# Causal attention over 1,024 rows: scores made once by query rows, four heads at a time, probabilities turned on TensorE

## The chip, the cores and the metric

The kernel runs on one core of a Trainium2 chip. The metric is device time in microseconds (us), the median of several executions. The core has TensorE (PE in the profile: matrix products and transposes, with weight loads listed as PEld), VectorE (DVE), ScalarE (ACT), GpSimd (POOL) and SyncE (SP, which here only issues DMAs). Each engine runs its own list of instructions strictly in the order written. Semaphores connect the lists.

## The reference, cut to what matters

```
x = L0_attn_x                                  # (4, 1024, 512)
xn = layernorm(x)
out = x + attn(xn) + ffn(xn)

def attn(x):                                   # 16 heads of 32
    q, k, v = split(x @ w_qkv)                 # 512 columns each
    q, k = rope(rmsnorm(q) * q_gamma), rope(rmsnorm(k) * k_gamma)
    scores = where(causal, q @ k.T / sqrt(32), -1e30)
    return (softmax(scores) @ v) @ w_out

def ffn(h):                                    # on 128 chosen rows of each batch
    idx = sort(top_k(h @ w_router, 128))
    x = h[idx]                                 # 512 rows in all
    ...                                        # attention of 16 heads of 128, and a gated MLP
    return h.at[idx].set(gate * processed + (1 - gate) * x)
```

## The kernel before, in words

The program has four stages on one core. First, rows are normalised and chosen for the FFN. Second, the attention of the chosen rows runs. Third comes their MLP, a loop of 16 steps in which PE is fed with weights split in a high and a low fp32r half. These three stages leave `delta`, what the FFN adds to its 512 rows. The fourth stage, which the change rewrites, is the attention over all 4 batches of 1,024 rows, written out by the functions `batch`, one for each engine.

For each batch PE first turns the normalised rows (L1154), and projects them tile by tile of 128 rows on q, k (L1176) and v (L1164) in plain fp32. DVE and POOL normalise and rope q and k: squares on ACT (L814), sums on DVE (L1479), the inverse root by a power on POOL (L597), scaling on DVE (L1490), and the sine products (L610 on POOL, L1502 on DVE). Then the tiles of the batch before get their output projection (`output`, L1097) plus one product with `onehotT` that puts `delta` on its rows (L1102).

The rest of a batch is a loop over 8 pairs of heads, each of 12 steps (`STEPS`), a step being a block of 128 keys against up to 512 queries. q and k are kept as stacks of a high part, a low part and a repeated high part, 96 rows (`STK`), so that one fp32r product has nearly fp32 precision. Row 97 of the q stack carries the negated row maximum. It is found one pair ahead, from scores made once more the other way round (`user` "max", L1079, seen by DVE at L1436 and L1440), turned on PE (L1084) and put in place by a small DMA. Scores then come out with keys on the partitions (L1118), ACT takes the exponent (L838), POOL blanks the part above the diagonal (L621), and PE multiplies by v and by ones in four column strips (L1142). DVE turns and inverts the sums and divides (L1449 to L1466). POOL splits the stacks of the pair after next (L578, L581), and PE turns them (L1072).

What runs beside a step is dealt out by the tables `BESIDE_Y` and `BESIDE_STEP`; banks of PSUM by `BANK`.

## Time and profile before

| | us |
|---|---|
| median of 3 runs | 1954.69 |
| lowest and highest run | 1952.83 and 1954.87 |
| profiled execution, first to last instruction (its span) | 1952.2 |
| PE busy in the span | 1766.3 |
| DVE busy | 1228.8 |
| ACT busy | 755.6 |
| POOL busy | 595.1 |

The page gives the profiled execution by its span. The runs are timed from outside the span, and the median stands 2.5 us above it. Busy time counts an engine's own instructions, and a matmul's entry reaches to its modelled end, so a full PE row does not mean that each column took the least time. What a matmul costs in a stream is read from the distance of starts.

### The profile page before, as it was taken

Reading aid. Unit: us, or ns where it says so; the run is one execution under the profiler, and the core shown is the slowest. Engines: PE = TensorE matmul, PEld = TensorE weight load, DVE = VectorE, ACT = ScalarE, POOL = GpSimd, SP = SyncE. Lnnn points to the kernel's source line nnn. Section 1 sums busy time; section 2 is a strip of 40 time slices with the busy share of each in tenths; the row PEclk is TensorE's granted clock in tenths of the full one; section 3 lists DMA queues with packets and bytes.
Section 4 is the critical chain, followed back from the end, with each engine's and each line's share of the span. In section 5 each row is a group of like instructions: output and inputs, shape, how many; then the busy total and the mean of one; then the engine's idle time right before and its main releaser. Section 6 shows DMA issues by size and latency. Waiting matters only on the chain.

```text
span 1952.2 us, 31482 instructions
## 1 busy us (share of the span) xinstructions
PE 1766.3 (90%) x9017; PEld 970.5 (50%) x9017; DVE 1228.8 (63%) x2797; ACT 755.6 (39%) x1682; POOL 595.1 (30%) x751
## 2 busy tenths in 40 slices
PE   0647999998998979999989999998999999899998
PEld 0435767666884445554435444444544444454443
DVE  6985656567984557775456777345677735467771
ACT  0002334332221126664124666312466531256652
POOL 1112010103443643331652332274233236422320
PEclk9878999999998969999999999999999999999999
DMA  7100112105331000001010000101000010100002
GB/s 249 54 1 22 33 32 64 32 16 180 99 104 43 0 1 2 2 2 44 1 54 34 2 2 2 45 1 54 34 2 2 2 46 0 65 23 2 2 2 87
DMA packets 55692, 70.43 MB, mean 36 GB/s; under 512 B 2680, under 2 KB 32048, under 8 KB 55536
## 3 DMA queue, kind: packets, MB, share of 16 engines
q1 hardware_dynamic: 55120, 67.20, 10.3%
q0 software_dynamic: 416, 1.34, 0.3%
q8 instruction: 75, 1.23, 0.3%
q14 instruction: 81, 0.66, 0.1%
HBM read 59.88 MB, written 8.39 MB: 35 GB/s over the span
## 4 chain that ended last, share of the span: by engine, by line
PE 71%; DVE 11%; ACT 7%; issue 7%; POOL 2%; DMA 1%; DVEq 0%; ACTq 0%; SPq 0%; POOLq 0%
PE psum L1142 13%; PE psum L1176 12%; PE psum L1079 9%; PE psum L1118 6%; PE psum L1097 5%; PE psum L1014 4%; PE psum L925 3%; PE psum L991 3%; ACT arena L838 3%; PE psum L1022 2%; PE psum L1072 2%; PE psum L935 2%; PE psum L969 2%; DVE arena L1490 2%; ACT k_stack L769 2%
## 5 line engine op out<-in xcount | busy, mean ns | idle before, releaser
L838 ACT ACTIVATE arena<-psum 128x512 f32<-128x512 f32 (+3 forms) x768 | 333.4, 488 | 247.0 <-PE psum L1118 245.9
L1440 DVE CUSTOM_DVE_ANT_0 psum<-psum,arena 128x128 f32<-128x128 f32 (+3 forms) x512 | 262.6, 527 | 211.3 <-PE psum L1079 205.8
L1142 PE MATMUL psum<-arena 128*32 128x512 f32 (+3 forms) x3072 | 326.1, 498 | 0.0
L1079 PE MATMUL psum<-k_stack,q_stack 96*128 96x512 f32 (+3 forms) x768 | 311.7, 438 | 11.3 <-ACT k_stack L769 7.6
L621 POOL TENSOR_SCALAR_AFFINE_SELECT arena<-arena 128x256 f32<-128x256 f32 x256 | 104.4, 408 | 498.7 <-ACT arena L838 498.7
L1079 PEld LDWEIGHTS psum<-k_stack,q_stack 96*128 96x128 f32 x768 | 139.2, 190 | 219.0 <-DVE arena L1436 72.6
L1176 PE MATMUL psum<-arena 128*128 128x512 f32 x512 | 227.2, 598 | 4.3 <-ACT arena L805 3.0
L1118 PE MATMUL psum<-q_stack,k_stack 97*128 97x512 f32 (+3 forms) x768 | 217.2, 364 | 0.2 <-DMA q_stack<-arena 0.2
L1436 DVE TENSOR_REDUCE arena<-psum 128x1 f32<-128x512 f32 x256 | 169.6, 687 | 28.4 <-PE psum L1079 28.2
L597 POOL TENSOR_TENSOR arena<-arena 128x32 f32<-128x32 f32 x32 | 173.8, 5431 | 2.8
L1176 PEld LDWEIGHTS psum<-arena 128*128 128x128 f32 x512 | 95.0, 190 | 134.2 <-issue 112.1
L1118 PEld LDWEIGHTS psum<-q_stack,k_stack 97*128 97x128 f32 x768 | 127.5, 190 | 49.5 <-ACT arena L838 37.1
L1097 PE MATMUL psum<-arena 128*128 128x512 f32 x256 | 132.9, 630 | 19.0 <-DVE arena L1490 16.4
L1072 PEld LDWEIGHTS psum<-ident_r,stack 128*96 128x96 f32 x1024 | 92.3, 127 | 93.4 <-issue 56.7
L1072 PE MATMUL psum<-ident_r,stack 128*96 128x128 f32 x1024 | 123.9, 246 | 12.5 <-POOL stack L581 12.4
L1506 DVE TENSOR_TENSOR arena<-arena 128x1024 f32<-128x1024 f32 x32 | 39.2, 1225 | 121.3 <-POOL arena L610 120.9
L1164 PE MATMUL psum<-arena 128*128 128x512 f32 x256 | 114.4, 592 | 0.0
L814 ACT ACTIVATE psum<-psum 128x1024 f32<-128x1024 f32 x32 | 32.3, 1008 | 210.8 <-PE psum L1176 210.8
L1479 DVE TENSOR_REDUCE arena<-psum 128x32 f32<-128x1024 f32 x32 | 39.2, 1224 | 97.1 <-ACT psum L814 97.1
L769 ACT ACTIVATE k_stack<-psum 96x512 fp32r<-96x512 f32 x128 | 77.6, 606 | 48.0 <-PE psum L1072 48.0
L527 POOL TENSOR_TENSOR k_stack<-arena,k_stack 128x512 fp32r<-128x512 f32 (+1 forms) x24 | 39.7, 1680 | 182.1 <-ACT k_stack L684 182.1
L1142 PEld LDWEIGHTS psum<-arena 128*32 128x32 f32 x3072 | 60.9, 108 | 67.1 <-issue 43.9
(161 smaller groups left out, 2562.3 us busy)
## 6 DMA issues: line engine op xcount, KB each, us to landing
arena<-in_L_attn_x SPq DMA_DIRECT2D x8, 2048.0 KB, 8.1
arena<-in_L_attn_x SPq DMA_DIRECT2D x16, 512.0 KB, 5.0
out_y<-arena SPq DMA_DIRECT2D x16, 512.0 KB, 2.7
arena<-in_L_ffn_wq SPq DMA_DIRECT2D x8, 512.0 KB, 4.5
arena<-in_L_ffn_wo SPq DMA_DIRECT2D x8, 512.0 KB, 4.0
arena<-in_L_ffn_w_gate SPq DMA_DIRECT2D x16, 256.0 KB, 2.9
arena<-in_L_ffn_w_up SPq DMA_DIRECT2D x16, 256.0 KB, 3.5
arena<-in_L_ffn_w_down SPq DMA_DIRECT2D x16, 256.0 KB, 2.6
```

Of the source, the lines that this page charges most:

```text
L597: pool.tensor_tensor(rs3[:, t % 2, :], ms3, half_neg, ALU.pow).then_inc(rs3_ready, 1)
L769: act.activation(dst, psum[0:RH, bank, :], ACT.Copy).then_inc(stackT_ready, 1)
L838: act.activation(probT[:, k % SLOTS, h, lo:CH], psum[:, (2 * k + h) % 3, lo:CH], ACT.Exp).then_inc(sc_exp, 1)
L1072: last = pe.transpose(psum[0:RH, bank, i * P:(i + 1) * P].bitcast(f32r), stack[:, w, t, h * STK:h * STK + RH], ident_r[:, :])
L1079: pe.matmul(psum[:, bank, 0:w], qS[p % 2][0:RH, t // 4, h * CH + t % 4 * P:h * CH + (t % 4 + 1) * P], kS[p % 2][0:RH, h, c * CH:c * CH + w ...
L1097: pe.matmul(bank, oT[:, g, t * P:(t + 1) * P], w_out[:, g, :], start=(g == 0), stop=False)
L1118: pe.matmul(psum[:, m % 3, lo:CH], kS[p % 2][0:RH + 1, h, j * P:(j + 1) * P], qS[p % 2][0:RH + 1, c, h * CH + lo:(h + 1) * CH], start=True ...
L1142: last = pe.matmul(psum[AD * r:AD * (r + 1), bank, lo:CH], w, probT[:, k % SLOTS, h, lo:CH], start=(j == 0), stop=(j == 4 * c + 3))
L1164: last = pe.matmul(psum[:, 4 + t % 2, :], xnT[:, k, t * P:(t + 1) * P], w_qkv[:, k, 2 * D:3 * D], start=(k == 0), stop=(k == KD - 1))
L1176: last = pe.matmul(psum[:, 2 * (t % 2) + w, :], xnT[:, k, t * P:(t + 1) * P], w_qkv[:, k, w * D:(w + 1) * D], start=(k == 0), stop=(k == K ...
L1436: dve.tensor_reduce(past, psum[:, bank, :], AX.X, ALU.max).then_inc(m_seen, 1)
L1440: dve.tensor_tensor_reduce(psum[:, bank, 0:w], psum[:, bank, 0:w], mask[:, CH - w:CH], 1.0, past if c else -3e38, ALU.add, ALU.max, top[:, ...
```

## The change

The last stage becomes 16 units (`U`), each a batch and four heads (`GH`). A unit has 24 pieces (`NPC`): for query tiles 0 to 3 two pieces of two heads each, for tiles 4 to 7 four pieces of one head. All engines walk the same loop over `i`, from `FIRST` (24 before the first piece) to `END`; the text calls a turn of it a slot, numbered 0 to 23 within its unit. In a slot:

- PE makes the scores of piece `i` with queries on the partitions, up to 1,024 keys wide, plus one product of `ident_r` with `limit` that sets the part above the diagonal (`score`). DVE takes the minimum of the negated scores (`least`), ACT the exponent with its sum (`probs`) into one of three `prob` buffers.
- PE turns the probabilities of piece `i - 2` in 128 x 128 blocks ("tA", "tB"), DVE and ACT copy them to `pT`.
- By the tables `STACK_AT`, `VALUE_AT`, `OUT_AT`, `XN_AT`, `QKV_AT` slots also hold the turned stacks of a coming query tile ("q", "k"), the values of a finished one ("o"), with the inverted sums spread by four more products, its output projection ("y", added by DVE to `y` in SBUF), for the first unit of a batch the turned x tiles ("x"), and one tile of the next unit's q, k, v projection ("w"). That projection is now three fp32r products of split operands, 384 columns wide. `w_qkv` is split by ACT and POOL during the MLP loop (`split_high`, `split_low`) and parked in DRAM.
- The next unit's q and k are normalised and roped in four chunks of two tiles: `rope3` on POOL, with the sums (`sums3`) and the scaling (`scale3`) on DVE in the slots of `SUMS_AT` and `SCALE_AT`.

The items "q" to "w" share four PSUM banks, dealt by `deal_banks`; `freed` makes PE wait until the item that had the bank before was read out. The product with `onehotT` goes; instead POOL adds `delta` to the rows of the output in DRAM by one indirect DMA for each batch, after the batch was written (`add_delta`). Loading x for the stage now waits until `delta` is done, since the memory is laid out anew.

```diff
+            def rope3(c):
+                u, cc = divmod(c, 4)
+                pool.wait_ge(raw_out, 2 * c + 2)
+                wait(pool, ss_made, c)
+                raw_c = raw3[:, c % 2].rearrange("p t n -> p (t n)")
+                pool.tensor_tensor(rot3, raw_c, raw_c, ALU.mult).then_inc(sq_made, 1)
+                pool.wait_ge(ss_made, c + 1)
+                wait(pool, rs_made, c)
+                pool.tensor_scalar(ms3, ss3[:, c % 2, :], 1.0 / AD, RMS_EPS, ALU.mult, ALU.add).then_inc(ms_made, 1)
+                pool.wait_ge(ms_made, c + 1)
+                pool.tensor_tensor(rs3[:, c % 2, :], ms3, half_neg[:, 0:16], ALU.pow).then_inc(rs_made, 1)
+                pool.wait_ge(scaled, c + 1)
+                wait(pool, lo_made, c)
+                src = raw3[:, c % 2].rearrange("p t (w h d) -> p (t w) h d", w=2, d=AD)
+                cos = cosG[:, 2 * cc:2 * cc + 2].rearrange("p t w d -> p (t w) d")
+                sin = sinG[:, 2 * cc:2 * cc + 2].rearrange("p t w d -> p (t w) d")
+                made = roped3.rearrange("p (a h d) -> p a h d", a=4, d=AD)
+                rot = rot3.rearrange("p (a h d) -> p a h d", a=4, d=AD)
+                half = AD // 2
+                pool.tensor_tensor(made, src, cos.unsqueeze(2).to_broadcast([P, 4, GH, AD]), ALU.mult)
+                for h in range(2):
+                    o = h * half
+                    last = pool.tensor_tensor(rot[:, :, :, o:o + half], src[:, :, :, half - o:AD - o],
+                                              sin[:, :, o:o + half].unsqueeze(2).to_broadcast([P, 4, GH, half]), ALU.mult)
+                last.then_inc(turned, 1)
+                pool.wait_ge(turned, c + 1)
+                pool.tensor_tensor(roped3, roped3, rot3, ALU.add).then_inc(roped_made, 1)
+                pool.wait_ge(roped_made, c + 1)
+                wait(pool, stack_ps, 2 * ((u - 1) * NT + 2 * cc + 2))
+                own = hl[:, 2 * cc:2 * cc + 2]
+                dst = own.rearrange("p t w h e d -> p (t w h) e d")
+                flat = roped3.rearrange("p (a d) -> p a d", d=AD)
+                parts = roped3.rearrange("p (t w h d) -> p t w h d", t=2, w=2, d=AD)
+                pool.tensor_copy(dst[:, :, 0, :], flat).then_inc(hi_made, 1)
+                for w in range(2):
+                    pool.tensor_copy(own[:, :, w, :, 2 - w, :], parts[:, :, w])
+                pool.wait_ge(hi_made, c + 1)
+                for w in range(2):
+                    last = pool.tensor_tensor(own[:, :, w, :, 1 + w, :], parts[:, :, w], own[:, :, w, :, 0, :].bitcast(f32), ALU.subtract)
+                last.then_inc(lo_made, 1)
...
+            def probs(i):
+                s, t, heads = piece(i)
+                w = (t + 1) * P
+                act.wait_ge(min_made, i + 1)
+                if i >= 3:
+                    act.wait_ge(tA_ps, i - 2)
+                    wait(act, tB_ps, seconds(i - 3))
+                wait(act, recip_made, s - 1)
+                for a, h in enumerate(heads):
+                    bank = 2 * (i % 2) + a
+                    src = psum[:, bank:bank + 2, :].rearrange("p a n -> p (a n)")[:, 0:w] if t >= 4 else psum[:, bank, 0:w]
+                    act.activation(prob[:, i % 3, a * CH:a * CH + w], src, ACT.Exp, bias=nmax[:, i % 4, a:a + 1], scale=-1.0,
+                                   accum_out=den[:, s % 2, h:h + 1]).then_inc(prob_made, 1)
...
+            def score(i):
+                s, t, heads = piece(i)
+                w = (t + 1) * P
+                wait(pe, prob_made, exps(i - 2))
+                pe.wait_ge(q_out, s + 1)
+                pe.wait_ge(k_out, s + 1)
+                for a, h in enumerate(heads):
+                    bank = 2 * (i % 2) + a
+                    if t >= 4:
+                        pe.matmul(psum[:, bank, :], qT[0:STK, s % 2, h, :], kT[0:STK, h, 0:CH], start=True, stop=True)
+                        bank, w0 = bank + 1, CH
                     else:
+                        w0 = 0
+                    pe.matmul(psum[:, bank, 0:w - w0], qT[0:STK, s % 2, h, :], kT[0:STK, h, w0:w], start=True, stop=False)
+                    last = pe.matmul(psum[:, bank, w - w0 - P:w - w0], ident_r[:, :], limit[:, :], start=False, stop=True)
+                last.then_inc(s_ps, 1)
...
+            def value(s):
+                u, t = divmod(s, NT)
+                bank = BANK_OF["o", s]
+                freed("o", s)
+                pe.wait_ge(recip_made, s + 1)
+                for h in range(GH):
+                    pe.matmul(psum[AD * h:AD * (h + 1), bank, P:2 * P], rden[:, s % 2, h:h + 1].to_broadcast([P, AD]), ident, start=True, stop=True)
+                pe.wait_ge(tA_out, end_of(s) + 1)
+                wait(pe, tB_out, seconds(end_of(s)))
+                pe.wait_ge(v_out, s + 1)
+                for j in range(t + 1):
+                    for h in range(GH):
+                        last = pe.matmul(psum[AD * h:AD * (h + 1), bank, 0:P], v[:, u % 2, j, h * AD:(h + 1) * AD], pT[:, s % 2, j, h, :],
+                                         start=(j == 0), stop=(j == t))
                 last.then_inc(o_ps, 1)
...
+            def project3(n):
+                u, m = divmod(n, NT)
+                bank = BANK_OF["w", n]
+                freed("w", n)
+                pe.wait_ge(w_in[u % 2], 16 * (u // 2 + 1))
+                pe.wait_ge(x_hi, u // 4 * NT + m + 1)
+                pe.wait_ge(x_lo, u // 4 * NT + m + 1)
+                for k in range(KD):
+                    for a, c in PARTS:
+                        last = pe.matmul(psum[:, bank, 0:3 * P], xnT[:, a, k, m * P:(m + 1) * P], w_s[u % 2][:, c, k, :],
+                                         start=(k == 0 and a + c == 0), stop=(k == KD - 1 and a == 1))
+                last.then_inc(w_ps, 1)
+            for i in range(FIRST, END):
...
+            def least(i):
+                s, t, heads = piece(i)
+                w = (t + 1) * P
+                bank = 2 * (i % 2)
+                dve.wait_ge(s_ps, i + 1)
+                if i >= 4:
+                    dve.wait_ge(prob_made, exps(i - 4))
+                if t < 4:
+                    dve.tensor_reduce(nmax[:, i % 4, :], psum[:, bank:bank + 2, 0:w], AX.X, ALU.min).then_inc(min_made, 1)
+                else:
+                    dve.tensor_reduce(nmax[:, i % 4, 0:1], psum[:, bank:bank + 2, :].rearrange("p a n -> p (a n)")[:, 0:w], AX.X, ALU.min).then_inc(min_made, 1)
...
+            def sums3(c):
+                dve.wait_ge(sq_made, c + 1)
+                wait(dve, rs_made, c - 1)
+                dve.tensor_reduce(ss3[:, c % 2, :], rot3.rearrange("p (h d) -> p h d", d=AD), AX.X, ALU.add).then_inc(ss_made, 1)
+            def scale3(c):
+                dve.wait_ge(rs_made, c + 1)
+                src = raw3[:, c % 2].rearrange("p t (h d) -> p (t h) d", d=AD)
+                dve.tensor_tensor(src, src, rs3[:, c % 2, :].unsqueeze(2).to_broadcast([P, 16, AD]), ALU.mult).then_inc(scaled, 1)
+            for i in range(FIRST, END):
+                if 0 <= i < U * NPC:
+                    least(i)
+                for kind, n in ring_items(i):
+                    if kind == "tA":
+                        first_out(n)
+                if recip_of(i) is not None:
+                    invert(recip_of(i))
+                for kind, n in ring_items(i - 1):
+                    if kind == "o":
+                        divide(n)
+                    if kind == "y":
+                        add_out(n)
+                    if kind == "x":
+                        x_low(n)
+                if turned_of(i, NORM_AT) is not None:
+                    normalise3(turned_of(i, NORM_AT))
+                if chunk_of(i, SUMS_AT, ()) is not None:
+                    sums3(chunk_of(i, SUMS_AT, ()))
+                if chunk_of(i, SCALE_AT, (0,)) is not None:
+                    scale3(chunk_of(i, SCALE_AT, (0,)))
...
+PROJECT, PROJECT_OUT, ROPE = (1, 3, 5), (2, 4, 6), (3, 5, 7)
+U = B * AH // 4
+GH = 4
+PIECES = [(t, (2 * a, 2 * a + 1)) for t in range(4) for a in range(2)] + [(t, (h,)) for t in range(4, NT) for h in range(GH)]
+NPC = len(PIECES)
+LAG = 2
+ENDS = [max(p for p in range(NPC) if PIECES[p][0] == t) for t in range(NT)]
...
+STACK_AT = {0: 1, 2: 2, 4: 3, 6: 4, 10: 5, 14: 6, 18: 7, 23: 8}
+VALUE_AT = {4: 0, 6: 1, 8: 2, 10: 3, 14: 4, 18: 5, 22: 6, 2: 7}
+OUT_AT = {6: 0, 8: 1, 10: 2, 12: 3, 16: 4, 20: 5, 0: 6, 4: 7}
+XN_AT = {1: 0, 2: 1, 4: 2, 6: 3, 8: 4, 10: 5, 12: 6, 15: 7}
+NORM_AT = {0: 0, 1: 1, 3: 2, 5: 3, 7: 4, 9: 5, 11: 6, 14: 7}
+QKV_AT = {3: 0, 5: 1, 7: 2, 9: 3, 11: 4, 13: 5, 16: 6, 19: 7}
+SUMS_AT = {7: 0, 11: 1, 15: 2, 21: 3}
+SCALE_AT = {10: 0, 14: 1, 18: 2, 0: 3}
+RECIP_AT = {3: 0, 5: 1, 7: 2, 9: 3, 13: 4, 17: 5, 21: 6, 1: 7}
...
+def ring_items(i):
+    s, out = stack_of(i), []
+    if s is not None:
+        out += [("q", s), ("k", s)]
+    if 0 <= i - LAG < U * NPC:
+        out.append(("tA", i - LAG))
+        if PIECES[(i - LAG) % NPC][0] > 1:
+            out.append(("tB", i - LAG))
+    for kind, n in (("o", value_of(i)), ("y", out_of(i)), ("x", turned_of(i)), ("w", projected_of(i))):
+        if n is not None:
+            out.append((kind, n))
     return out
...
+FIRST, END = -NPC, U * NPC + 6
+HELD = {"q": 0.6, "k": 0.8, "tA": 0.7, "tB": 0.6, "o": 1.5, "y": 1.5, "x": 1.5, "w": 1.0}
+def deal_banks():
+    free, holder, bank_of, before = [0.0] * 4, [None] * 4, {}, {}
+    for i in range(FIRST, END):
+        items = ring_items(i)
+        for n, (kind, idx) in enumerate(items):
+            k = min(range(4), key=lambda m: free[m])
+            bank_of[kind, idx] = 4 + k
+            before[kind, idx] = holder[k]
+            holder[k] = (kind, idx)
+            free[k] = i + n / max(4, len(items)) + HELD[kind]
+    return bank_of, before
+BANK_OF, BEFORE = deal_banks()
```

**DVE, between the scaling of one piece of q and k and the sums of the next.** Before, tile by tile in the projection, where `sums(t + 1)` stands ahead of the scaling of tile t:

```order
L1479 TENSOR_REDUCE arena<-psum 128x32 [waits ms3_ready,qk_sq]
L1490 TENSOR_TENSOR arena<-psum,arena 128x1024 [waits rs3_ready]
L1497 TENSOR_TENSOR arena<-arena 128x512 [waits scaled]
L1497 TENSOR_TENSOR arena<-arena 128x512
L1502 TENSOR_TENSOR arena<-arena 128x16x16 x2
L1506 TENSOR_TENSOR arena<-arena 128x1024 [waits cosed,rotated]
```

Now, from `scale3` of chunk 0 in slot 10 to `sums3` of chunk 1 in slot 11 of a unit:

```order
L1460 TENSOR_TENSOR raw<-raw,rs 128x512 [waits rs_made]
L1399 TENSOR_REDUCE nmax<-psum 128x1 [waits prob_made,s_ps]
L1412 COPY pT<-psum 128x4x128 [waits o_ps,tA_ps]
L1424 TENSOR_TENSOR oT<-psum,rdT 128x128 [waits y_ps,rdT_made]
L1434 TENSOR_TENSOR y<-psum,y 128x512 [waits y_added,y_ps]
L1454 TENSOR_REDUCE ss<-rot 128x16 [waits rs_made,sq_made]
```

The sums stood ahead of the scaling and waited for ACT's squares. They now stand one slot behind the scaling of the chunk before and wait for `sq_made`, POOL's squares.

**POOL, one tile of rope before, one chunk now.** Before:

```order
L595 TENSOR_SCALAR arena<-arena 128x32 [waits scaled,rs3_ready,ss3_ready]
L597 TENSOR_TENSOR arena<-arena 128x32 [waits ms3_ready]
L610 TENSOR_TENSOR arena<-arena 128x16x16 [waits roped_ready,scaled]
L610 TENSOR_TENSOR arena<-arena 128x16x16
```

Now, from the moment that a chunk is scaled to the power of the next chunk:

```order
L615 TENSOR_TENSOR roped<-raw,cosG 128x512 [waits lo_made,scaled]
L618 TENSOR_TENSOR rot<-raw,sinG 128x16x16 x2
L622 TENSOR_TENSOR roped<-roped,rot 128x512 [waits turned]
L629 CAST hl<-roped 128x16x32 [waits roped_made]
L631 CAST hl<-roped 128x2x4x32 x2
L634 TENSOR_TENSOR hl<-roped,hl 128x2x4x32 [waits hi_made]
L634 TENSOR_TENSOR hl<-roped,hl 128x2x4x32
L601 TENSOR_TENSOR rot<-raw 128x512 [waits ss_made,raw_out]
L604 TENSOR_SCALAR ms<-ss 128x16 [waits rs_made,ss_made]
L606 TENSOR_TENSOR rs<-ms,half_neg 128x16 [waits ms_made]
```

POOL had two sine products between a scaling and its next power. It now has the whole rope and the split of the stacks, eight instructions, and then the squares of the next chunk for which DVE waits.

**PE, a place in the loop over steps before, and slot 14 now.** Before:

```order
L1118 MATMUL psum<-q_stack,k_stack 128x512
L1079 MATMUL psum<-k_stack,q_stack 128x512
L1079 MATMUL psum<-k_stack,q_stack 128x128
L1142 MATMUL psum<-arena 32x512 x4
L1084 MATMUL psum<-arena 8x128
```

Now:

```order
L1085 MATMUL psum<-kT,qT 128x512
L1089 MATMUL psum<-kT,qT 128x256
L1090 MATMUL psum<-limit,ident_r 128x128
L1118 MATMUL psum<-ident_r,hl 96x128 x8
L1108 MATMUL psum<-consts,prob 128x128 x6
L1128 MATMUL psum<-consts,rden 32x128 x4
L1134 MATMUL psum<-pT,v 32x128 x20
```

Products of 512 columns in the strips (32 weight columns) gave way to products of 128 columns, and turned probabilities (L1108) stand where the second scores (L1079) stood.

## Rows read from the trace of the kernel before

**Rows 1.** The page, part 1: busy us, share of the span, instructions.

```profile
PE 1766.3 (90%) x9017; PEld 970.5 (50%) x9017; DVE 1228.8 (63%) x2797; ACT 755.6 (39%) x1682; POOL 595.1 (30%) x751
```

**Rows 2.** The chain that ended last, in time: start us, us, what, instructions.

```profile
207.16 5.31 PE psum L935 x48
...
459.93 2.75 PE psum L1014 x12
...
600.82 2.41 DVE arena L1399 x4
...
917.37 14.01 PE psum L1176 x32
...
1586.19 14.01 PE psum L1176 x32
...
1918.16 3.43 PE psum L1097 x8
```

**Rows 3.** Windows: length, busy us and count by engine, then PE's granted clock.

```profile
700.00:731.00 31.00, 21.62 (x88) 14.11 (x88) 19.96 (x50) 11.86 (x28) 10.45 (x17) 0.50 0.00 1
...
1055.00:1239.90 184.90, 182.43 (x1342) 88.81 (x1344) 130.72 (x348) 116.57 (x281) 51.27 (x111) 1.00 0.01 3
1240.20:1250.00 9.80, 6.26 (x29) 4.96 (x28) 2.35 (x4) 3.52 (x6) 0.81 (x4) 0.65 0.03 8
```

**Rows 4.** Timeline of PE inside a pair: start us, us.

```profile
1101.67 0.48 PE L1072 MATMUL psum<-ident_r,stack 128*96 128x128 f32 x4
1101.99 0.58 PE L1118 MATMUL psum<-q_stack,k_stack 97*128 97x384 f32 x2
...
1102.75 0.43 PE L1142 MATMUL psum<-arena 128*32 128x128 f32 x8
1103.11 0.48 PE L1072 MATMUL psum<-ident_r,stack 128*96 128x128 f32 x4
```

**Rows 5.** Timeline of PE, the last three steps of strips (384, 256, 128 columns).

```profile
1907.98 1.50 PE L1142 MATMUL psum<-arena 128*32 128x384 f32 x24
```

**Rows 6.** Timeline of PE, eight fp32 transposes in a row.

```profile
161.56 1.03 PE L885 MATMUL psum<-arena 128*128 128x128 f32 x8
```

**Rows 7.** Groups of DVE by shape: busy us, mean ns, idle before.

```profile
L1436 DVE TENSOR_REDUCE arena<-psum 128x1 f32<-128x512 f32 x256 | 169.6, 687 | 28.4 <-PE psum L1079 28.2
...
L1479 DVE TENSOR_REDUCE arena<-psum 128x32 f32<-128x1024 f32 x32 | 39.2, 1224 | 97.1 <-ACT psum L814 97.1
```

**Rows 8.** Groups of ACT by shape.

```profile
L838 ACT ACTIVATE arena<-psum 128x512 f32<-128x512 f32 x384 | 206.8, 590 | 141.6 <-PE psum L1118 141.3
...
L814 ACT ACTIVATE psum<-psum 128x1024 f32<-128x1024 f32 x32 | 32.3, 1008 | 210.8 <-PE psum L1176 210.8
...
L702 ACT ACTIVATION_READ_ACCUMULATOR arena<-arena 128x1 f32 x64 | 12.1, 190 | 0.0
```

**Rows 9.** Groups of POOL by shape.

```profile
L597 POOL TENSOR_TENSOR arena<-arena 128x32 f32<-128x32 f32 x32 | 173.8, 5431 | 2.8
...
L581 POOL TENSOR_TENSOR stack<-arena,stack 128x256 fp32r<-128x256 f32 x120 | 86.6, 742 | 9.5 <-POOL stack L578 8.2
L610 POOL TENSOR_TENSOR arena<-arena 128x256 f32<-128x256 f32 x64 | 49.1, 787 | 9.9 <-DVE arena L1490 9.9
L578 POOL CAST stack<-arena 128x256 fp32r<-128x256 f32 x120 | 45.0, 404 | 155.5 <-PE psum L1072 147.1 <-DVE arena L1506 8.4
L533 POOL TENSOR_TENSOR k_stack<-arena,k_stack 128x512 fp32r<-128x512 f32 x32 | 41.0, 1305 | 61.6 <-ACT k_stack L730 61.6
...
L494 POOL TENSOR_TENSOR arena<-arena 128x8 f32<-128x8 f32 x4 | 6.8, 1702 | 0.3
```

**Rows 10.** The page, part 6: DMA issues, KB each, us to landing.

```profile
arena<-in_L_attn_x SPq DMA_DIRECT2D x8, 2048.0 KB, 8.1
...
out_y<-arena SPq DMA_DIRECT2D x16, 512.0 KB, 2.7
```

1043 lines of the change are left out of this document (429 added, 614 removed).

## The prediction

> **What bounds the kernel now.** I read the page first for who is busy, then the chain that ended last for where time goes, then windows and a close timeline for what a product costs. PE is busy for 1766 of 1952 us, DVE for 1229 [rows 1]. The chain says where the last stage begins: DVE ends its last sum at 600.8 + 2.4 = 603.2 us, so the rewritten stage has 1349 of the 1952 us, and a batch costs (1586.2 - 917.4) / 2 = 334.4 us [rows 2]. In the pairs of a batch PE is busy for 182.4 of 184.9 us [rows 3]. So PE bounds the stage, and the question is whether it gets less to do and still gets it in time. Busy time doesn't tell the first, since an entry lasts longer than its place in a stream. I price PE by distances of starts.
>
> **Prices on PE.** An fp32r product of 512 columns costs 2.75 / 12 = 0.229, one of 128 costs 5.31 / 48 = 0.111 [rows 2]; between them I interpolate at the same slope (256: 0.122, 384: 0.176). An fp32 product of 512 columns is two instructions of 3.43 / 8 = 0.429, together 0.858 [rows 2]. Eight fp32 transposes end within 1.03 [rows 6]; without the last one's drain that is near the 0.111 of a 128-column product with its own weight load, and I take 0.11. Four fp32r transposes of a stack start 0.32 before what follows [rows 4]. Four strips of 128 columns (eight instructions) hold PE for 1103.11 - 1102.75 = 0.36 when they stand alone [rows 4]. Three steps in a row with 768 columns end within 1.50, or 1.43 without the 0.07 by which the entry in rows 4 outlasts its place; so each further 128 columns cost (1.43 - 0.36) / 5 = 0.21 [rows 5]. I take 0.22 and keep 0.36 as the other bound.
>
> How much the prices leave out I read from the pairs: scores 8 x 4.4, second scores and turned stacks 7 x 6.7, strips 8 x 10.5 make about 169 us, and with 184.9 us for some 430 groups of instructions [rows 3] a change of group costs 0.036.
>
> **PE's work in one of the 16 units.** Scores: 4 heads x (8 x 0.111 for the diagonal, 4 x 0.229, twice 0.638 for the odd widths) = 12.3. Turned probabilities: 36 blocks x 4 heads x 0.11 = 15.8. Turned stacks: 16 x 0.32 = 5.1. Values: 8 groups, 8 x 0.36 + 36 x 0.22 = 10.8, with the spread sums as one block each. Output: 8 x 0.858 = 6.9. Projection: 8 tiles x 12 x 0.176 = 16.9. Turned x: 0.9 on average. That is 68.7 us, and 118 groups x 0.036 = 4.2 beside. Four units make 292 us against the 334.4 of a batch now. By PE's work alone the change wins 12% of the stage: it drops the second scores and ones, and three fp32r products replace four passes of fp32, which outweighs the turned probabilities.
>
> **What the other engines have to do in a unit.** DVE: a reduction costs 0.687 at 512 and 1.224 at 1,024 [rows 7], so 0.15 + 1.05 per 1,000 columns; 24 minima over 18,432 columns are 23 us, 24 copies out 15.7, the rest 16, together 55. ACT: 0.17 + 0.82 per 1,000 columns, and 0.19 for reading each sum [rows 8]: 32 exponents 27 to 30, copies 26, together 55. POOL: a chunk of `rope3`. A 512-wide product costs 1.31, a 256-wide one 0.74 to 0.79, a cast of 256 0.40 and so of 512 about 0.67, and the power 1.70 for 8 and 5.43 for 32, so 2.95 for 16 [rows 9]. None of them is above PE's 73 in sum. The order is what matters.
>
> **The wait that the order makes.** After `scale3` of a chunk POOL must do the cosine product 1.3, two sine products 1.6, the sum 1.3, the cast 0.67, two copies 0.8, two subtractions 1.5, and only then the squares of the next chunk, 1.3, in all 8.8 with 0.35 for its own waits. `sums3` of the next chunk needs those squares, and stands on DVE one slot behind the scaling, for chunks 1 (slot 11 after 10) and 2 (slot 15 after 14). A slot of PE is 2.9 us on average. DVE has four instructions there, 2.5 us. So DVE stands still for 5 to 6 us twice a unit. Queued behind the sums are `least` and `first_out` of the next slot: ACT's exponents wait for the first, PE's banks for the second.
>
> I walked PE, DVE and ACT from there with the prices above and `deal_banks`' order. Time 0 is the end of the sums in slot 11. While DVE stood, PE did slot 12 and the start of 13 and then stopped, because "tB" of slot 13 lies in the bank of "tA" of slot 12, not copied yet: 3.6 us lost. DVE then needs 7.1 us to reach the scaling in slot 14; the squares and sums take 9.5; PE meanwhile ends slot 16 and stops before "tA" of slot 17, whose bank again waits for `first_out`: 4.3 us lost. Then 5.6 us to the scaling in slot 18, and 10.4 to the sums in slot 21, which find their squares ready, since three slots lie between. From there PE leads: its slots 22 to 9 are 35.7 us of work, group changes 2.2, x 0.5, 2.1 for slots 7 and 9, in which "w" takes the bank of the same slot's "tA" and waits for `least` and the copy; slot 10 up to its scaling 3.0, less 2.6 that PE was ahead: 40.9. And 9.6 back to time 0. The circle is 7.1 + 9.5 + 5.6 + 10.4 + 40.9 + 9.6 = 83.1 us a unit. Checked from PE's side: 68.7 + 4.2 + 7.9 + 2.9 for banks (the two slots above, and slot 11) = 83.7.
>
> **The ends.** The stage may load x only once `delta` is made: 603.2 + 1.9 for four multiplications that before came after the first normalised tile. What goes from the row choice (the turned one-hot matrix, about 2 us of PE and ACT) and what the splitting of `w_qkv` adds to the MLP loop (ACT and POOL have gaps there, but the chain through DVE is tight: 0 to 6 us) I set against each other. x and the first 1.5 MB of weights land about 8.3 us later, from 8.1 for 2 MB [rows 10]: 613.5. Two tiles projected at the 1.2 GHz that a pause leaves (half clock, as in [rows 3]) and copied out: 8.1, so 621.6. Squares and sums 2.1, then three chunks of 13.7 (power 3.2, scaling 0.7, 8.8, sums 0.7, handovers 0.3), since DVE reaches slot 0 only after the sums of chunk 3: 664.8. From the like point of unit 14 there are 2.9 us to its end. Unit 15 projects nothing: 50.9 + 4 for groups + 4 for banks and slots too short for DVE and ACT = 59. Its tail (last copies, values, division, projection) is 8, the output lands in 2.7 [rows 10], and the indirect DMA, for which no row exists, I set at 5, between 2.7 and 9: together 16.
>
> **Sum.** 664.8 + 15 x 83.1 + 2.9 + 59 + 16 = 1989 us of span, against 1952.2; with the 2.5 us by which the median of the runs stands above the span, 1992. The change is even with the kernel before at (1952.2 - 664.8 - 77.9) / 15 = 80.6 us a unit. Each us in a unit is 15 in the whole.
>
> **Rivals.** (1) Faster, because DVE's stop is covered: if PE runs further ahead than I let it, or POOL's eight steps take less. Half of the 7.9 us saved gives 79.1 a unit and 1932; all of it leaves 68.7 + 4.2 + 3.4 = 76.3 and 1890. It decides from 1.25 us less in each of the two gaps. For it: POOL's rows hold waits for the port and for data, DVE's are means over longer chains. Against it: POOL's products lie close to 0.74 and 1.31 in 120 and 32 instances [rows 9], and five of the eight steps are chained. Chance 0.33, faster in each form.
>
> (2) Slower still, because the clock falls in the gaps. The clock was at half for 31 us when PE was busy for 21.6 of them, and 0.65 in the 9.8 us that begin with a pause of 3.5 us and go on with 28 transposes [rows 3]. The gaps here are 3.6 and 4.3 us. One such fall in a unit, 6.8 us at half speed, costs 3.4, so 51 us: 2043. Against it: the gaps hold parts of products of 384 columns at both sides. Chance 0.17. The Trainium skill (TensorE: Matmul & The Clock Gate, Part 4: PE-mode transpose) states that transposes don't count as a busy PE in the way products do. [...] By that rule 21 of the 68.7 us would not count here, and the fall would be likelier.
>
> (3) Slower, because small strips don't stream: weights of 32 columns are loaded for each 128 columns, not for 512. At 0.36 for every block a unit costs 5.0 more: 2072. For it: the only steps in a row in the trace are wide ones [rows 5]. Chance 0.10.
>
> **How the numbers follow.** My own case holds 0.40, with 1965 to 2020 from POOL's chain at 8.0 to 9.5. The range 1885 to 2075 takes in the covered case at its lower end and the third rival at its upper end and leaves about 0.2 out. About 0.2% is what a measurement of this kernel can tell from no change. Faster 0.34, within 0.2% 0.04, slower 0.62.
>
> **What would show it.** In the changed kernel's trace DVE's sums (L1454) wait for POOL's squares (L601) by 5 to 6 us, twice a unit, and PE has gaps of about 4 us before L1108 in slots 13 and 17. Units come every 83 us. Strips (L1134) start 0.22 apart per block. If the sums wait for less than 2 us, the second part of my argument is wrong, and the time is near 1900.

## The result, and the profile after

The changed kernel takes 2020.19 us, the median of 5 runs from 2008.11 to 2025.24, against 1954.81 for the kernel before. The ratio is 1.0334, 95% interval 1.0305 to 1.0363: slower by 3.3%. The forecast was 1992, range 1885 to 2075, with a chance of 0.62 for slower; the median lies at the upper end of what the forecast gave its own case (1965 to 2020). The profiled execution is the shortest of the five (2008.11 us, span 2006.2). That matters below.

The page of the changed kernel, parts 1 and 5, answers to [rows 1] and [rows 7, 9]:

```profile
PE 1675.8 (84%) x14233; PEld 1366.2 (68%) x14233; DVE 1241.0 (62%) x2293; ACT 927.1 (46%) x2363; POOL 865.4 (43%) x940
...
L615 POOL TENSOR_TENSOR roped<-raw,cosG 128x512 f32<-128x512 f32 x64 | 81.6, 1275 | 323.5 <-DVE raw L1460 323.5
...
L606 POOL TENSOR_TENSOR rs<-ms,half_neg 128x16 f32<-128x16 f32 x64 | 186.4, 2913 | 5.3
...
L1454 DVE TENSOR_REDUCE ss<-rot 128x16 f32<-128x512 f32 x64 | 43.6, 682 | 161.4 <-POOL rot L601 161.4
```

PE is busy for 90 us less than before, and the whole is longer. DVE's sums stood still for 161.4 us behind POOL's squares. No share in part 1 shows it: POOL is busy 43% of the time. It is late at two places in each unit. The table of waits gives the number of times and the longest, and what came of it on PE:

```profile
DVE ss L1454 <- POOL rot L601: 161.4, 34, 7.8
...
PE psum L1108 <- DVE pT L1412: 92.6, 54, 3.7
...
PE psum L1166 <- DVE pT L1412: 53.2, 42, 6.3
```

One unit's second wait, on the timeline of DVE (start us, us, and idle time before it in brackets):

```profile
1141.04 0.68 DVE L1460 TENSOR_TENSOR raw<-raw,rs 128x512 f32<-128x512 f32 x1
1142.71 0.96 DVE L1399 TENSOR_REDUCE nmax<-psum 128x1 f32<-128x768 f32 x1 [0.99 <-PE psum L1090]
1143.59 0.68 DVE L1412 COPY pT<-psum 128x512 f32<-128x512 f32 x1
1144.18 0.28 DVE L1424 TENSOR_TENSOR oT<-psum,rdT 128x128 f32<-128x128 f32 x1
1149.58 0.69 DVE L1454 TENSOR_REDUCE ss<-rot 128x16 f32<-128x512 f32 x1 [5.12 <-POOL rot L601]
```

POOL in the same stretch starts the cosine product when the scaling has ended, and is busy without a gap until the squares end:

```profile
1141.81 1.27 POOL L615 TENSOR_TENSOR roped<-raw,cosG 128x512 f32<-128x512 f32 x1 [5.16 <-DVE raw L1460]
1143.04 1.42 POOL L618 TENSOR_TENSOR rot<-raw,sinG 128x256 f32<-128x256 f32 x2
1144.54 1.26 POOL L622 TENSOR_TENSOR roped<-roped,rot 128x512 f32<-128x512 f32 x1
1145.86 0.61 POOL L629 CAST hl<-roped 128x512 fp32r<-128x512 f32 x1
1146.42 0.74 POOL L631 CAST hl<-roped 128x256 fp32r<-128x256 f32 x2
1147.12 1.43 POOL L634 TENSOR_TENSOR hl<-roped,hl 128x256 fp32r<-128x256 f32 x2
1148.51 1.04 POOL L601 TENSOR_TENSOR rot<-raw 128x512 f32<-128x512 f32 x1
```

PE meanwhile ends slot 16 and the scores of slot 17 and stops. The first line is its stop in slot 13, behind the first wait, the second the one in slot 17:

```profile
1134.88 0.33 PE L1108 MATMUL psum<-consts,prob 128*128 128x128 f32 x1 [2.00 <-DVE pT L1412]
...
1151.92 0.87 PE L1108 MATMUL psum<-consts,prob 128*128 128x128 f32 x6 [3.63 <-DVE pT L1412]
```

Windows show the clock behind each gap (length, busy us by engine with counts; PE's granted clock is the third number from the end, as in [rows 3]):

```profile
1135.70:1139.10 3.40, 3.40 (x12) 3.30 (x11) 1.25 (x3) 1.32 (x4) 0.94 (x1) 0.50 0.00 0
1152.80:1156.20 3.40, 3.40 (x22) 2.71 (x25) 3.02 (x7) 2.55 (x7) 0.75 (x1) 0.50 0.00 0
...
1112.80:1194.90 82.10, 73.37 (x754) 62.65 (x753) 48.27 (x82) 47.28 (x125) 42.97 (x48) 0.96 0.06 21
```

Both stretches of 3.4 us run at half clock, 1.2 GHz, with PE busy all the time. That is 6.8 us of this unit of 82.1. So each unit has the wait that I forecast, and behind it a good part of rival (2).

In what follows, a unit is the distance from the sums of one unit's first chunk to the next one's, and a mean is over units 1 to 14. In the changed kernel it is 84.65 us. Plain units (2, 6, 14) take 82.0, with one stretch at half clock less (unit 10) 80.5, the second of each batch (1, 5, 9, 13) 82.5 to 84.6, and the six in which x is turned (3, 4, 7, 8, 11, 12) 85.8 to 88.0. Of the mean 10.4 us are gaps of PE over 0.3 us and 6.6 us are at half clock.

### The profile page after: what moved, and what is told of

The parts are those of the page before. It is cut to its first block, busy times and chain, and to the rows that moved or that the text cites. A ratio compares the mean times of both kernels' runs of the same rounds, so it can differ in the third digit from the quotient of the medians.

```text
span 2006.2 us, 40434 instructions
## 1 busy us (share of the span) xinstructions
PE 1675.8 (84%) x14233; PEld 1366.2 (68%) x14233; DVE 1241.0 (62%) x2293; ACT 927.1 (46%) x2363; POOL 865.4 (43%) x940
## 4 chain that ended last, share of the span: by engine, by line
PE 59%; DVE 15%; POOL 13%; issue 8%; ACT 2%; DMA 1%; DVEq 0%; POOLq 0%; ACTq 0%; SPq 0%
PE psum L1166 12%; PE psum L1108 8%; PE psum L1134 5%; PE psum L1145 4%; PE psum L1118 3%; PE psum L1089 3%; PE psum L935 3%; DVE pT L1412 3%; PE psum L1001 3%; POOL rot L618 2%; POOL hl L634 2%; POOL roped L622 2%; POOL roped L615 2%; PE psum L1085 2%; PE psum L1024 2%
## 5 line engine op out<-in xcount | busy, mean ns | idle before, releaser
L819 ACT ACTIVATE prob<-psum,nmax 128x896 f32<-128x896 f32 (+7 forms) x512 | 376.1, 739 | 196.3 <-DVE nmax L1399 157.3
L1108 PE MATMUL psum<-consts,prob 128*128 128x128 f32 x2304 | 345.9, 283 | 94.4 <-DVE pT L1412 92.6
L1399 DVE TENSOR_REDUCE nmax<-psum 128x1 f32<-128x640 f32 (+3 forms) x256 | 261.4, 1021 | 226.4 <-PE psum L1090 226.3
L1166 PE MATMUL psum<-w_s,xnT 128*128 128x384 f32 x1536 | 328.6, 366 | 79.9 <-DVE pT L1412 53.2
L1166 PEld LDWEIGHTS psum<-w_s,xnT 128*128 128x128 f32 x1536 | 285.0, 203 | 102.9 <-DVE pT L1412 64.9
L1108 PEld LDWEIGHTS psum<-consts,prob 128*128 128x128 f32 x2304 | 252.9, 144 | 117.7 <-DVE pT L1412 110.1
L1412 DVE COPY pT<-psum 128x512 f32<-128x512 f32 (+1 forms) x320 | 214.4, 670 | 21.0 <-PE psum L1108 19.6
L606 POOL TENSOR_TENSOR rs<-ms,half_neg 128x16 f32<-128x16 f32 x64 | 186.4, 2913 | 5.3
L1089 PE MATMUL psum<-kT,qT 96*128 96x384 f32 (+3 forms) x512 | 177.7, 369 | 1.4 <-ACT kT L796 0.8
L1134 PE MATMUL psum<-pT,v 128*32 128x128 f32 x4608 | 149.4, 273 | 0.0
L1454 DVE TENSOR_REDUCE ss<-rot 128x16 f32<-128x512 f32 x64 | 43.6, 682 | 161.4 <-POOL rot L601 161.4
L1145 PE MATMUL psum<-w_out,oT 128*128 128x512 f32 x256 | 140.0, 629 | 3.2 <-ACT qT L791 1.0
L1085 PE MATMUL psum<-kT,qT 96*128 96x512 f32 x256 | 137.1, 536 | 0.1
```

Source lines behind the costliest of these rows:

```text
L606: pool.tensor_tensor(rs3[:, c % 2, :], ms3, half_neg[:, 0:16], ALU.pow).then_inc(rs_made, 1)
L819: act.activation(prob[:, i % 3, a * CH:a * CH + w], src, ACT.Exp, bias=nmax[:, i % 4, a:a + 1], scale=-1.0, accum_out=den[:, s % 2, h:h + ...
L1085: pe.matmul(psum[:, bank, :], qT[0:STK, s % 2, h, :], kT[0:STK, h, 0:CH], start=True, stop=True)
L1089: pe.matmul(psum[:, bank, 0:w - w0], qT[0:STK, s % 2, h, :], kT[0:STK, h, w0:w], start=True, stop=False)
L1108: last = pe.transpose(psum[:, bank, n * P:(n + 1) * P], prob[:, i % 3, a * CH + j * P:a * CH + (j + 1) * P], ident)
L1134: last = pe.matmul(psum[AD * h:AD * (h + 1), bank, 0:P], v[:, u % 2, j, h * AD:(h + 1) * AD], pT[:, s % 2, j, h, :], start=(j == 0), stop= ...
```

## The experiments

Each was run beside the kernel before on the same chip; medians of 4 to 10 runs, ratios with 95% interval. The kernel before had a median of 1953.3 to 1954.8 beside each, so the times can be compared with each other. The last three columns are from one trace each.

| | us | ratio | unit | gaps | at half clock |
|---|---|---|---|---|---|
| changed kernel | 2020.19 | 1.0334 [1.0305, 1.0363] | 84.65 | 10.4 | 6.6 |
| sums later | 1890.63 | 0.967 [0.9654, 0.9686] | 76.75 | 5.0 | 1.2 |
| squares early | 1964.31 | 1.0052 [1.0032, 1.0071] | 81.17 | 7.7 | 3.4 |
| one more product on POOL | 2068.66 | 1.0579 [1.0562, 1.0597] | 88.33 | 12.6 | 11.7 |
| gaps filled | 2007.83 | 1.0275 [1.0258, 1.0292] | 84.34 | 6.3 | 2.4 |
| sums later, one more product | 1896.26 | 0.9709 [0.9692, 0.9725] | 76.41 | 5.0 | 0.5 |
| sums later, w before tB | 1896.42 | 0.97 [0.9684, 0.9716] | 76.89 | 4.2 | 0 |
| sums later, plain fp32 w | 1951.31 | 0.9988 [0.9978, 0.9998] | 80.50 | 4.9 | 1.0 |
| sums later, banks at start | 1884.26 | 0.9655 [0.9639, 0.9672] | 76.55 | 5.0 | 0.7 |
| first unit early | 1876.18 | 0.9598 [0.9582, 0.9614] | 76.61 | 4.5 | 2.0 |

**The wait taken away by two tables.**

```diff
-SUMS_AT = {7: 0, 11: 1, 15: 2, 21: 3}
-SCALE_AT = {10: 0, 14: 1, 18: 2, 0: 3}
+SUMS_AT = {7: 0, 12: 1, 17: 2, 22: 3}
+SCALE_AT = {9: 0, 14: 1, 19: 2, 0: 3}
```

> Only the two tables are changed: the sums of a chunk stand at slots 7, 12, 17, 22 in place of 7, 11, 15, 21, and the scalings at 9, 14, 19 and 0 in place of 10, 14, 18 and 0. Between a scaling and the next sums there are then three slots, about 9 us, where there was one. No work is added or taken out. Theory (the queue of DVE waits for POOL's squares): the sums wait for less than 1 us each, the gaps of 2.0 and 3.6 us before the turned probabilities of slots 13 and 17 go, and with them the stretches at half clock behind them. A unit falls from 84.65 us (mean of units 1 to 14) by 5.6 us of gap and about half of the 6.6 us at half clock, so to 76 to 78 us; the span falls from 2006 to 1880 to 1905 us. Rival (the bound is PE's own work and the four banks, and the waits of DVE only show where slack lies): the gaps reopen at other banks, a unit stays above 82 us, and the time above 1965 us.

1890.63 us, 6.4% below the changed kernel and 3.3% below the one before. The waits of the sums fall from 161.4 us in 34 places to 26.7 in 18 (in units 1 to 14 from 132.9 to 14.4); the gaps of slots 13 and 17 are gone. A plain unit (unit 2) in the windows:

```profile
765.80:839.40 73.60, 69.79 (x754) 60.00 (x753) 48.08 (x82) 47.70 (x126) 42.95 (x48) 1.00 0.06 23
```

The clock is full, and the engines do what they did before in 82.1 us (754 matmul entries in both). So the work of the change was never the trouble. By the prices of the prediction about 21 us of this unit are transposes, mixed with products, and the clock stays at 2.4 GHz. The Trainium skill (TensorE: Matmul & The Clock Gate, Part 4: PE-mode transpose) states that transposes don't count as a busy PE in the way products do. Nothing of that shows here, nor in the kernel before, where PE does nothing but fp32 transposes (L1154) from 1243.74 to 1250.85 and the clock rises from half to full among them:

```profile
1243.70:1249.60 5.90, 5.86 (x25) 4.69 (x26) 0.00 (x0) 3.12 (x6) 0.00 (x0) 0.50 0.02 4
1249.60:1250.90 1.30, 1.13 (x8) 0.69 (x7) 0.00 (x0) 1.09 (x3) 0.00 (x0) 0.99 0.00 0
```

The transposes start 0.213 us apart before 1249.6 and 0.110 after it. The changed kernel has the same transposes in a unit, and gaps of 2 and 3.6 us beside them, and there the clock falls. With the gaps filled, further down, it nearly stops falling: the fall hung on the gaps.

**The wait shortened by POOL's order.** In `rope3`, for chunks 0 and 1 (the squares go into `roped3`, and the rope waits until they are summed):

```diff
+                if cc in (0, 1):
+                    squares(c + 1)
+                    pool.wait_ge(ss_made, c + 2)
                 pool.wait_ge(scaled, c + 1)
```

> The tables of the changed kernel stay. On POOL the squares of chunks 1 and 2 are issued ahead of the rope and stack split of the chunk before (into the buffer of the roped values, so that the rope starts only when the sums have been made). Theory (DVE's queue waits for POOL's chain): the sums in slots 11 and 15 find their squares ready. But now rope and split (8.0 us) and the power (3.2 us) lie between the sums in slot 11 and the scaling in slot 14, and again between 15 and 18, where PE needs some 9 to 10 us; so part of the wait, 1.5 to 2.5 us each, comes back at the scalings. A unit takes 79 to 82 us against 84.65, the whole 1920 to 1965 us. If the order on POOL doesn't matter (rival: PE's work and banks), the unit stays within 1 us of 84.65.

1964.31 us. As expected the wait moves. The table of waits, where L1466 is now the sums and L1472 the scaling:

```profile
DVE ss L1466 <- POOL rot L604: 26.7, 16, 7.8
...
DVE raw L1472 <- POOL rs L615: 77.3, 30, 9.5
```

In units 1 to 14 alone the scaling waits for 56.1 us in 25 places, 2.2 us each, where the sums had waited for 4.7; that is within the 1.5 to 2.5 expected. The unit takes 81.17 us and the whole 56 us less than the changed kernel, at the upper edge of what was expected. The order on POOL counts, but chain and slots still don't fit until the slots are moved.

**The wait made longer.** One product `rot3 = roped3 * roped3` on POOL behind the split of chunks 0 and 1.

> One useless product of 512 columns, 1.07 to 1.3 us, is added on POOL to the changed kernel behind the stack split of chunks 0 and 1 of each unit, so that the squares for slots 11 and 15 come that much later. POOL is busy for 43% of the span, so by its busy share this costs nothing. Theory: each us is one us of the unit, twice: 2.1 to 2.6 us a unit, 32 to 39 us in the whole, so 2050 to 2060 us. Rival (the waits of DVE are covered by other work): under 8 us in the whole.

2068.66 us: 48.5 more, above the range, and 3.7 a unit where 2.1 to 2.6 were expected. The distance from scaling to sums grew by 1.1 and 1.2 us, which is the part that I had, and PE's gaps by 2.2 us a unit. The rest goes with the clock: 11.7 us at half in a unit in place of 6.6, which at 0.33 a us (the next experiment) is 1.7 us.

**The gaps filled.** In `score`, ahead of the true products:

```diff
+                    for _ in range({13: 8, 17: 14}.get(i % NPC, 0)):
+                        pe.matmul(psum[:, bank, :], qT[0:STK, s % 2, h, :], kT[0:STK, h, 0:CH], start=True, stop=True)
```

> PE repeats a product of 512 columns of its scores 8 times in slot 13 and 14 times in slot 17, about 1.8 and 3.2 us of useless work, ahead of the gaps of 2.0 and 3.6 us in which it waits for the copy out of a bank. DVE stands at the sums meanwhile, so what it waits for doesn't come later. This tells the clock from the wait. If the half clock for 3.4 us behind each gap is caused by the gap and costs time, the stretches at half clock in slots 13 to 18 go and a unit falls by 2 to 3.3 us, in the whole 30 to 50 us, to 1970 to 1990 us, although PE does 80 us more work. If the clock costs nothing beside the wait, the time stays within 8 us of the changed kernel, or rises by up to 15 us where the filler outlasts a gap.

2007.83 us. The sums still wait 161.2 us in 36 places, so the wait is as it was, and the timeline of PE shows the fillers (L1085 here) and what is left of the second gap:

```profile
1151.24 3.35 PE L1085 MATMUL psum<-kT,qT 96*128 96x512 f32 x14
...
1155.51 0.87 PE L1110 MATMUL psum<-consts,prob 128*128 128x128 f32 x6 [0.45 <-DVE pT L1414]
```

In 11 of the 14 units the stretches at half clock nearly go (6.5 to 0.3 us) and a unit falls by 2.0 us on the mean, 83.8 to 81.7: each us at half clock had cost 0.33. In the other 3 (4, 8 and 12, in which x is turned in slots 8 to 15) PE stops sooner behind the second wait, before the projection of slot 16. The fillers of slot 17 stand behind that gap and fill nothing:

```profile
985.32 4.21 PE L1168 MATMUL psum<-w_s,xnT 128*128 128x384 f32 x12 [6.30 <-DVE pT L1414]
989.33 4.28 PE L1085 MATMUL psum<-kT,qT 96*128 96x512 f32 x14
```

These units got 4 to 8 us longer. The whole therefore fell by only 12 us, which neither of the two expectations had (30 to 50, or within 8); the clean part of the evidence is the 11 units.

**The same kernel once more.**

> The changed kernel as it is, one more execution with its trace. The five executions took 2008 to 2025 us with mean clocks of 0.943 to 0.932, and the trace read so far is the shortest of them. If the difference is the clock behind the gaps, this trace has gaps of the same length at the same slots, and a span over 2006 us goes with more time at half clock: by the 1.3 us that a stretch of 3.4 us cost in the run with filled gaps, 12 us more in the span go with some 32 us more at half clock, mean clock 0.934 to 0.937. If it is something else (DMA, waits), the time at half clock is the same and the gaps differ.

Span 2021.8 at a clock of 0.933. PE's waits are the same, here for units 1 to 14 of the second look and then of the first:

```profile
PE psum L1108 <- DVE pT L1412: 85.0, 48, 3.7
PE psum L1166 <- DVE pT L1412: 50.4, 39, 6.3
```

```profile
PE psum L1108 <- DVE pT L1412: 84.9, 48, 3.7
PE psum L1166 <- DVE pT L1412: 50.5, 39, 6.3
```

A clock of c over a span means 2 x (1 - c) of it at half: 271 us here, 229 in the first. 42 us more at half clock, 15.6 us more in the span. Of this 24 and 10.4 us lie in units 1 to 14, and 22 and 5 us in the start of the stage, up to the first sums of unit 1 (603.2 to 689.0 in the first look); what stands ahead of 603.2 takes the same time in both, with 5 us less at half in the second. So with the same gaps the clock falls more often in one execution than in another, and that goes with the scatter of the five runs of the changed kernel over 17 us (mean clock 0.943 to 0.932). Those of the kernel before scatter over 2.5.

Within one trace it is the same. In unit 10 of the changed kernel the gap of slot 13 was followed by full clock:

```profile
1474.38 0.33 PE L1108 MATMUL psum<-consts,prob 128*128 128x128 f32 x1 [2.03 <-DVE pT L1412]
```

```profile
1474.40:1490.60 16.20, 12.47 (x120) 10.91 (x121) 9.13 (x14) 7.74 (x21) 11.57 (x13) 1.00 0.01 2
```

And units 4 and 8 of the kernel with the later sums have the same gaps, 6.04 us in all, but 6.8 us at half clock in the first and none in the second:

```profile
917.90:1000.00 82.10, 75.56 (x771) 64.62 (x770) 51.87 (x88) 49.97 (x129) 47.48 (x54) 0.96 0.21 73
1227.70:1306.70 79.00, 72.46 (x770) 61.58 (x769) 51.87 (x88) 49.99 (x129) 47.50 (x54) 1.00 0.23 76
```

3.1 us for 6.8 at half, 0.45 a us.

**POOL's extra product with slack.** The same product, on top of the later sums.

> The useless product on POOL behind chunks 0 and 1 (the one that took the changed kernel from 2020 to 2069 us) is added to the kernel with the later sums (1890.6 us). In its trace 11.65 us lie between the scaling of chunk 0 and the sums of chunk 1 and 9.54 between the next two, and POOL's squares need 8.5. Theory: the first of the two products is covered, the second has 1.0 us of cover for 1.07 to 1.3 us and may cost 0.3; in the whole 0 to 6 us, 1890 to 1897 us. Rival (POOL's work costs time by itself, by the port that it shares with DVE or by PE's waits for stacks): 15 us or more.

1896.26 us. A plain unit takes 73.59 in place of 73.57: nothing, where the same product had cost 3.7. The 5.6 us come from the start, where nothing covers the product: unit 0's last sums stand 7.7 us later (676.8 in place of 669.1). Units 1 to 14 give 4.7 us back in this trace, with 0.5 us at half clock in a unit in place of 1.2.

**What bounds it then.** The projection as one plain product on the high parts, which leaves out the low parts:

```diff
-                    for a, c in PARTS:
-                        last = pe.matmul(psum[:, bank, 0:3 * P], xnT[:, a, k, m * P:(m + 1) * P], w_s[u % 2][:, c, k, :], ...
+                    last = pe.matmul(psum[:, bank, 0:3 * P], xnT[:, 0, k, m * P:(m + 1) * P].bitcast(f32), w_s[u % 2][:, 0, k, :].bitcast(f32), ...
```

> The tables of the experiment with the later sums (1890.6 us), with the projection made by one plain fp32 product of 384 columns in place of three fp32r products (it leaves out the low parts, so the values are rougher). By the distances of starts a plain product of 384 columns takes two instructions of 0.32 us, 0.644, and three fp32r ones 3 x 0.174 = 0.522; 32 such groups in a unit give 3.9 us. If PE is now the bound, the whole rises by 16 x 3.9 = 62 us, to 1945 to 1960 us. If DVE's queue or POOL's chain still sets the pace, by less than 20 us.

1951.31 us: 60.7 more, for 62 expected, and 77.50 in a plain unit in place of 73.59, 3.9 as expected. With the wait gone PE is the bound, and the split projection alone is worth nearly all that separates the kernel with the later sums from the one before.

**A gap that only moves.** In `ring_items`, for slots that have both, "w" is put ahead of "tB".

> The tables of the experiment with the later sums (1890.6 us), and in slots that have both, the projection w stands ahead of the turned probabilities tB. In the trace of that experiment PE still has gaps of 1.13, 0.61 and 0.94 us before L1166 in slots 7, 9 and 11 of each unit, where w gets the bank that tA of the same slot had, not yet copied. Now tB gets that bank, and the 2.1 us of w lie between. If these gaps cost their length, a unit falls by 2 to 2.7 us and the whole to 1848 to 1862 us. Rival: PE gains nothing, since exponents and copies of the next slots then come 2.1 us later and PE waits for them; 1880 to 1900 us.

1896.42 us, 5.8 more: the rival. The timeline of PE with the later sums, and then with w ahead:

```profile
838.64 2.35 PE L1166 MATMUL psum<-w_s,xnT 128*128 128x384 f32 x12 [1.13 <-DVE pT L1412]
```

```profile
844.55 1.09 PE L1108 MATMUL psum<-consts,prob 128*128 128x128 f32 x8 [0.18 <-ACT pT L805]
846.33 0.42 PE L1128 MATMUL psum<-consts,rden 128*32 128x128 f32 x8 [0.69 <-ACT v L844]
```

The wait of 1.13 us for DVE's copy became waits of 0.18 and 0.69 one slot later, for the copy of "tB" and for ACT's copy of v, which it makes last in its slot while the next "o" has been dealt that bank. With gaps under 0.3 us counted in, PE is idle for 3.8 us of a plain unit in both kernels. Yet such a unit takes 74.57 in place of 73.59; where PE's stream loses this 1 us I have not looked.

**The start.** In `deal_banks`, `free` begins at `float(FIRST)` and not at 0.0.

> The kernel with the later sums (1890.6 us), and in deal_banks the banks are free from FIRST on, not from 0. Slots of the first projection are numbered -24 to -1, below the 0.0 with which the banks begin, so that every x and w there gets bank 4: a tile then takes 6.6 us in a row (turn, copy out, three products, copy out) in the trace of that kernel, for 52 us. With four banks the turn of a tile runs beside the projection of the one before. Theory: a tile takes 4 to 5 us, the first chunk is scaled about 3 to 4 us sooner, and then POOL's chain of 12.5 us a chunk sets the pace as before; the whole falls by 3 to 8 us, to 1883 to 1888 us. Rival: POOL's chain is not the bound and the whole gain of some 15 us arrives: 1875 us or less. Steady units don't change.

1884.26 us, 6.4 less. The timeline of PE before and after this edit:

```profile
634.60 3.92 PE L1166 MATMUL psum<-w_s,xnT 128*128 128x384 f32 x12 [1.41 <-DVE xnT L1440]
639.16 0.65 PE L1153 MATMUL psum<-consts,xs 128*128 128x128 f32 x4 [0.64 <-ACT v L844]
```

```profile
625.53 0.63 PE L1153 MATMUL psum<-consts,xs 128*128 128x128 f32 x4
625.92 2.36 PE L1166 MATMUL psum<-w_s,xnT 128*128 128x384 f32 x12
```

A tile takes 2.6 us there and no longer 6.6: it doesn't wait for a bank, and the clock is full (2.36 and 3.92 us for the same 12 products). The clock's part isn't the edit's alone: in the trace of the changed kernel, with the same waits, it was full from 620.3 on, and a tile took 5.1 us. Yet the last sums come only 5.9 us sooner, since POOL's chain goes on at 12.5 us a chunk. So the next one lets unit 0 begin with two chunks:

```diff
+SUMS_AT = {9: 0, 13: 1, 0: 2, 5: 3}
+SCALE_AT = {10: 0, 15: 1, 2: 2, 6: 3}
+QKV_AT = {3: 0, 5: 1, 7: 2, 9: 3, 11: 4, 13: 5, 17: 6, 21: 7}
```

(slots 0 and 5 of the sums and 2 and 6 of the scalings belong to the unit that runs)

> The bank change of the run before, and new tables: sums at slots 9, 13, and 0 and 5 of the unit that uses them, scalings at 10, 15, 2 and 6, projected tiles 6 and 7 in slots 17 and 21 in place of 16 and 19. Between a scaling and the next sums there are again 8.5 to 12 us everywhere. So unit 0 can begin when two of its four chunks are scaled and not three. Theory: slot 0 of unit 0 begins 15 to 18 us sooner than at 664.7, and the stop of 4.3 us behind its first scores shrinks; steady units stay at 76 to 77.5 us. The whole: 1862 to 1876 us. Rival: the tables are tight at other places (the scaling in slot 6 stands 3.7 us behind the sums in slot 5, and ACT waits for raw's buffer in slots 11 and 17), a unit takes 1 us more or worse, and the gain of the start is given back: 1885 us or more.

1876.18 us, at the upper edge of what I expected. Unit 0 begins at 652.8 in place of 664.6, 11.8 us sooner and not 15 to 18; the stop behind its first scores is 1.1 us in place of 4.3; plain units take 72.98, but those in which x is turned 81 to 82 in place of 78.6 to 82.1. This is the best version: 4.0% below the kernel before, 7.1% below the changed one.

## Why the prediction was right, point by point

**The mechanism** was as told: sums one slot behind a scaling, POOL's eight steps between, `first_out` queued behind the sums, PE stopped before L1108 in slots 13 and 17 (in 3 of 14 units in slot 16, before L1166). Taken away, it gives 130 us.

**The chain on POOL.** I had 8.8 us from the end of the scaling to the end of the squares, and 9.5 to the end of the sums. In the unit shown it is 7.8 (1141.72 to 1149.55) and 8.55, one us less; counted from the start of the scaling, 9.2. The power of 16 columns, interpolated at 2.95, takes 2.91; the squares 1.04, not 1.3.

**The waits and gaps.** DVE waits 4.7 us on the mean in units 1 to 14, for 5 to 6. The gap in slot 17 is 3.6 for 4.3 (6.3, in slot 16, in three units). That in slot 13 is 2.0 in seven units, 3.5 in four and 1.1 in three, for 3.6: PE was less far ahead than my walk had it. Together the two are 6.5 us of a mean unit, for 7.9; the other gaps over 0.3 us are 3.9, for 2.9 of banks. The sum, 10.4 for 10.8, agrees better than its parts do, which is luck.

**PE's prices.** A unit without gaps over 0.3 us and without the clock's cost is 84.65 - 10.4 - 2.2 = 72.1 us, for 68.7 + 4.2 = 72.9. The 4.2 rests on a slip: 8 x 4.4, 7 x 6.7 and 8 x 10.5 make 166 us and not 169. With 166 a change of group is 0.044 and 118 of them are 5.2, and the price would have been 73.9, 1.8 us too high. The strips settle rival (3). Two steps of 5 and 6 blocks in the changed kernel:

```profile
1140.79 1.27 PE L1134 MATMUL psum<-pT,v 128*32 128x128 f32 x40
1141.99 0.50 PE L1085 MATMUL psum<-kT,qT 96*128 96x512 f32 x1
...
1156.33 1.48 PE L1134 MATMUL psum<-pT,v 128*32 128x128 f32 x48
1157.75 0.50 PE L1085 MATMUL psum<-kT,qT 96*128 96x512 f32 x1
```

The next products start 1.20 and 1.42 us behind the first strip, so each further block costs 0.22, as priced, and the first 0.32.

**The ends.** Up to the end of the first unit's last sums I had 664.8, and it is 667.5. Two errors offset each other. The first sums end at 628.7 and not 623.7: `delta` is made at 607.2, 4.0 us behind 603.2 where I had 1.9, and the first tiles go through one bank (with the banks free from the start the first sums came 2.7 us sooner). And the three chunks behind them take 38.8 us and not 41.1, as POOL's chain is shorter. From the last sums to the end there are 77.8 us, for 77.9; of this the end of the indirect DMA, set at 5, took 6.2 (2000.0 to 2006.2), and what stands before it was 1 us shorter than priced.

**The sum.** 667.5 + 15 x 84.06 + 77.8 = 2006.2, for 664.8 + 15 x 83.1 + 77.9 = 1989. The step that was short is the unit, by 1.0 us, and it is the clock: I had left rival (2) out of my own case as an alternative, and it belongs in it. It costs about 0.33 x 6.6 = 2.2 us a unit (3.0 at 0.45 a us), which cheaper work (0.8) and smaller gaps (0.4) partly offset, so that 83.1 came out only 1.0 short. It also goes with the median standing 14 us above the traced span and not 2.5: the other runs had a mean clock of 0.932 to 0.937, this one 0.943. Of the 28 us between 1992 and 2020, 17 are the trace's and 11.5 this.

**Rival (1)** did not happen in the changed kernel, but its price was about right. I gave 76.3 us a unit and 1890 with DVE's stop wholly covered; the later sums gave 76.75 and 1890.6. That the whole agrees to 1 us is luck: up to unit 0's last sums there are 669.8 us and not 664.8, behind the last ones 75.3 and not 77.9 (they stand a slot later now), and the median stands 0.3 above the traced span.

**Rival (2)** had the size of the half clock right, 6.8 us a unit for 6.6, and its price too high, 0.5 a us. Its argument for a likelier fall, by which the transposes would not count, is not borne out by the kernel before at 1243.7 to 1250.9 (see the first experiment).

## What to carry to other kernels

A stage written as one list of slots is as fast as its tightest pair of slots, not as its busiest engine. For each hand-over between two engines, add up the steps in between and count the slots that it is given: 8.5 us from a scaling to the squares that follow, nearly all of it POOL's, in a slot of 3 us cost more here than all that was saved on PE, while the same chain with three slots cost nothing, even 1 us longer. And when PE stops because of it, count the clock too, as a part of the wait and not as another case.
